# The attention output is turned by DMA transposes of a float16 pair instead of by TensorE

## The reference

```python
# layer 0
q = jnp.einsum('qc,bcn->bqn', Wq, xf)
k = jnp.einsum('qc,bcn->bqn', Wk, xf)
v = jnp.einsum('vc,bcn->bvn', Wv, xf)
attn = jax.nn.softmax(jnp.einsum('bqn,bqm->bnm', q, k) * scale, axis=-1)
out = jnp.einsum('bvm,bnm->bvn', v, attn).reshape(b, c, h, w)
y = gamma[0] * jnp.einsum('oc,bchw->bohw', Wo, out) + x
# layer 1, on y cut into 8 x 8 patches p
low = p.reshape(B * nP, C, 4, 2, 4, 2).mean(axis=(3, 5))
high = p - _up2_nearest(low)
low = _prelu(_bn(einsum('oc,nchw->nohw', mag_w, low) + mag_b), alpha)
hs = jnp.concatenate([high, jnp.roll(high, 1, axis=2)], axis=1)
hs = _prelu(_bn(einsum('oc,nchw->nohw', phase_w, hs) + phase_b), alpha)
out = _up2_nearest(low) + hs[:, :C]
```

## Time and profile before

| | us |
|---|---|
| median of 3 runs (2370.53 to 2370.84) | 2370.56 |
| span of the profiled execution | 2369.9 |
| PE busy | 2294.1 (97%) |
| DVE busy | 1784.5 (75%) |
| ACT busy | 1369.1 (58%) |
| POOL busy | 720.0 (30%) |

### The profile page before, as it was taken

The page is one execution under the profiler, slowest core; times in us unless marked ns, Lnnn a source line. Parts: engine busy times, 40 slices in busy tenths (PEclk is TensorE's granted clock), DMA queues, the critical chain, the costliest instruction groups (busy, mean ns, idle before and its releaser), DMA issues.

```text
span 2369.9 us, 48520 instructions
## 1 busy us (share of the span) xinstructions
PE 2294.1 (97%) x16885; PEld 1845.1 (78%) x16885; DVE 1784.5 (75%) x2838; ACT 1369.1 (58%) x2547; POOL 720.0 (30%) x891
## 2 busy tenths in 40 slices
PE   5799999999989999999999999999999999999997
PEld 4588888887878888888877888878887777777786
DVE  6777887777777777887776877777887777778764
ACT  3456665555655656665655655656665555565564
POOL 2232332232332232332232323232332223133222
PEclk7899999999999999999999999999999999999998
DMA  4201110000110001110000100000000000000000
GB/s 155 66 19 40 40 40 31 31 28 30 40 41 32 30 19 40 40 40 31 31 27 23 31 31 31 13 18 31 31 31 22 22 12 9 21 21 21 21 18 19
DMA packets 42119, 75.50 MB, mean 32 GB/s; under 512 B 4864, under 2 KB 6144, under 8 KB 42080
## 3 DMA queue, kind: packets, MB, share of 16 engines
q1 hardware_dynamic: 42080, 75.00, 9.8%
HBM read 55.59 MB, written 19.40 MB: 32 GB/s over the span
## 4 chain that ended last, share of the span: by engine, by line
PE 91%; issue 4%; DVE 2%; ACT 1%; POOL 1%; DMA 0%; SPq 0%; DVEq 0%; ACTq 0%; POOLq 0%
PE O L521 19%; PE O L523 18%; PE O L522 18%; PE M L374 14%; PE M L411 10%; PE S L482 10%; PE M L392 1%; ACT p L641 1%; DVE pl L899 1%; PE M L417 1%; DMA uh<-in_x 0%; DVE on L894 0%; POOL z L1052 0%; PE O L374 0%; ACT ph L638 0%
## 5 line engine op out<-in xcount | busy, mean ns | idle before, releaser
L521 PE MATMUL O<-uh,ph 128*128 128x257 f16 x4096 | 1136.0, 277 | 2.3 <-DVE pl L899 1.9
L523 PE MATMUL O<-uh,pl 128*128 128x257 f16 x4096 | 1122.6, 274 | 0.0
L522 PE MATMUL O<-ul,ph 128*128 128x256 f16 x4096 | 1119.8, 273 | 0.0
L638 ACT ACTIVATE ph<-S 128x512 f16<-128x512 f32 x1024 | 612.3, 598 | 705.0 <-PE S L482 704.4
L814 DVE TENSOR_REDUCE pmax<-M 128x1 f32<-128x512 f32 (+1 forms) x1024 | 679.7, 686 | 329.1 <-PE M L411 317.1
L899 DVE TENSOR_TENSOR pl<-p,ph 128x512 f16<-128x512 f32 x1024 | 782.1, 764 | 136.6 <-ACT p L641 131.3
L641 ACT ACTIVATE p<-S 128x512 f32<-128x512 f32 x1024 | 609.3, 595 | 0.8 <-DVE pl L899 0.2
L521 PEld LDWEIGHTS O<-uh,ph 128*128 128x128 f16 x4096 | 401.0, 98 | 263.2 <-issue 142.5
L482 PE MATMUL S<-qcur,kst 128*128 128x512 f32 x1024 | 486.0, 479 | 21.7 <-ACT p L641 16.9
L523 PEld LDWEIGHTS O<-uh,pl 128*128 128x128 f16 x4096 | 401.9, 98 | 51.2
L522 PEld LDWEIGHTS O<-ul,ph 128*128 128x128 f16 x4096 | 405.1, 99 | 38.9
(11 more groups left out here) (147 smaller groups left out, 1702.5 us busy)
## 6 DMA issues: line engine op xcount, KB each, us to landing
xr<-in_x SPq DMA_DIRECT2D x37, 512.0 KB, 3.6
out_y<-z SPq DMA_DIRECT2D x32, 512.0 KB, 2.8
xb<-in_x SPq DMA_DIRECT2D x25, 512.0 KB, 3.6
xs<-in_x SPq DMA_DIRECT2D x21, 512.0 KB, 3.7
qraw<-q_scratch SPq DMA_DIRECT2D x99, 64.0 KB, 1.8
ul<-in_x SPq DMA_DIRECT2D x4, 512.0 KB, 8.1
uh<-in_x SPq DMA_DIRECT2D x4, 512.0 KB, 8.7
q_scratch<-qsave SPq DMA_DIRECT2D x32, 64.0 KB, 1.6
```

Source lines behind the costliest of these rows:

```text
L521: nc.tensor.matmul(O[j][:, 0:UW], ph[:, t % 4, q], uh[parity][:, t, :], start=(t == 0), stop=False)
L522: nc.tensor.matmul(O[j][:, 0:C], ph[:, t % 4, q], ul[parity][:, t, :], start=False, stop=False)
L523: ins = nc.tensor.matmul(O[j][:, 0:UW], pl[:, t % 4, q], uh[parity][:, t, :], start=False, stop=(t == MT - 1))
L638: nc.scalar.activation(ph[:, t % 4, :], S[t % 2][:, :], ACT.Exp, scale=SCALE)
```

## The change

`normalise` writes the output as a float16 pair. `onh` is `oraw` times the reciprocal of the sum, rounded; `onl` is the same product less `onh`, rounded. The gain per image is no longer multiplied into `rs` but copied to `gcur`. A new `turn_out` on SP waits for the pair and issues two DMA transposes, `onh` to `yth` and `onl` to `ytl`, each of 128 x 1024 elements of two bytes, eight blocks of 128 x 128. They stand between the load of `xb` and the load of `xr`. The `y` tasks are gone from all plans and from PE. `add_residual` is now one block on DVE behind the tasks of step 6 (`RESIDUAL`): it waits for the transposes, multiplies `yth` by the gain and adds `xr` in two instructions, waits for these, and adds `ytl` times the gain in two more. Who waited for the `y` tasks (POOL's frequency split and SP's load of `xr`) waits for `y_ready`. Two output weights that were loaded through `on` get a buffer `wraw` of their own.

```diff
-FULL = Plan(steps_with_maxima({0: [("kq",), ("u", 0)], 2: [("u", 1)], 5: [("y", 0)], 6: [("y", 1)], 19: [("low", 0)],
+FULL = Plan(steps_with_maxima({0: [("kq",), ("u", 0)], 2: [("u", 1)], 19: [("low", 0)],
...
+            def turn_out(g):
+
+                sp.wait_ge(on_ready, g + 2)
+                sp.sem_inc(on_seen, 1)
+                for src, dst in ((onh, yth), (onl, ytl)):
+                    sp.dma_start_transpose(dst[:, :, :, :].rearrange("p j t q -> p (j t) q"),
+                                           src[:, :, :].rearrange("p j c -> p (j c)")).then_inc(on_turned, 16)
...
-                emptied(sp, plan, g, ("y", 1))
+                turn_out(g)
+                sp.wait_ge(y_ready, g + 1)
...
-                nc.vector.tensor_tensor(rs[:, :], rs[:, :], gain.to_broadcast([128, SUB]), ALU.mult).then_inc(rs_step, 1)
+                for j in range(SUB):
+                    ins = nc.vector.tensor_scalar(onh[:, j, :], oraw[:, j, 0:C], rs[:, j:j + 1], None, ALU.mult)
+                ins.then_inc(rs_step, 1)
+                nc.vector.tensor_copy(gcur[:, :], gain)
                 dve.wait_ge(rs_step, 2 * g + 2)
                 for j in range(SUB):
-                    ins = nc.vector.tensor_scalar(on[:, j, :], oraw[:, j, 0:C], rs[:, j:j + 1], None, ALU.mult)
+                    ins = nc.vector.scalar_tensor_tensor(onl[:, j, :], oraw[:, j, 0:C], rs[:, j:j + 1], onh[:, j, :],
+                                                         ALU.mult, ALU.subtract)
                 ins.then_inc(on_ready, 1)
...
+            def add_residual(g):
+
+                dve.wait_ge(on_turned, 32 * g + 32)
+                dve.wait_ge(xr_loaded, 16 * g + 16)
+                dve.wait_ge(high_ready, g + 1)
+                yv = [y[:, h, :, :].rearrange("p r w -> p (r w)").rearrange("p (j q) -> p j q", q=128) for h in range(CT)]
+                for h in range(CT):
+                    ins = nc.vector.scalar_tensor_tensor(yv[h], yth[:, :, h, :], gcur[:, 0:1],
+                                                         xr[:, h, :].rearrange("p (j q) -> p j q", q=128), ALU.mult, ALU.add)
+                ins.then_inc(y_half, 1)
+                dve.wait_ge(y_half, g + 1)
+                for h in range(CT):
+                    ins = nc.vector.scalar_tensor_tensor(yv[h], ytl[:, :, h, :], gcur[:, 0:1], yv[h], ALU.mult, ALU.add)
+                ins.then_inc(y_ready, 1)
...
+                    if t == RESIDUAL:
+                        add_residual(g)
```

More of the change, by code:

```diff
@@ L42 @@
 LEAD = 2
-ROUND_X, ROUND_CONV, SCAN, NEGATIVE = 9, 14, 12, 26
+ROUND_X, ROUND_CONV, SCAN, NEGATIVE, RESIDUAL = 9, 14, 12, 26, 6
 DOUBLE = (8, 10, 14, 16, 18, 22, 24, 26)
@@ L76, in steps_with_maxima @@
     return steps
-FULL = Plan(steps_with_maxima({0: [("kq",), ("u", 0)], 2: [("u", 1)], 5: [("y", 0)], 6: [("y", 1)], 19: [("low", 0)],
+FULL = Plan(steps_with_maxima({0: [("kq",), ("u", 0)], 2: [("u", 1)], 19: [("low", 0)],
                                20: [("low", 1)], 21: [("high", 0)], 23: [("high", 1)]}))
-LAST = Plan(steps_with_maxima({4: [("y", 0)], 5: [("y", 1)], 19: [("low", 0, 1)], 21: [("high", 0)], 23: [("high", 1)]},
+LAST = Plan(steps_with_maxima({19: [("low", 0, 1)], 21: [("high", 0)], 23: [("high", 1)]},
                               first=3, doubled=(6, 8, 10, 12, 14, 16, 18, 24, 25)),
             before=(FULL, ALL - NCH))
-FINAL = Plan({4: [("y", 0)], 5: [("y", 1)], 19: [("low", 0)], 20: [("low", 1)], 21: [("high", 0)], 23: [("high", 1)]},
+FINAL = Plan({19: [("low", 0)], 20: [("low", 1)], 21: [("high", 0)], 23: [("high", 1)]},
              before=(LAST, NCH - 1))
-TAIL = Plan({0: [("y", 0), ("y", 1), ("low", 0), ("low", 1), ("high", 0), ("high", 1)]}, before=(FINAL, 1))
+TAIL = Plan({0: [("low", 0), ("low", 1), ("high", 0), ("high", 1)]}, before=(FINAL, 1))
 MAXIMA_BY_KEYS = [(j, m) for m in range(NCH) for j in range(SUB)]
@@ L150, in attention_conv @@
         rs = sb("rs", [128, SUB])
-        on = sb("on", [128, SUB, C])
+        wraw = sb("wraw", [128, SUB, C])
+        onh, onl = [sb(n, [128, SUB, C], f16) for n in ("onh", "onl")]
+        yth, ytl = [sb(n, [128, SUB, CT, 128], f16) for n in ("yth", "ytl")]
+        gcur = sb("gcur", [128, 1])
         y = sb("y", [128, CT, ROWS, WID])
@@ L164, in attention_conv @@
         wraw_v = p32[:, 1, :].rearrange("p (t n) -> p t n", n=C)
-        wraw_o = on[:, 0:CT, :]
-        wraw_qk = on[:, CT:2 * CT, 0:2 * DQK]
+        wraw_o = wraw[:, 0:CT, :]
+        wraw_qk = wraw[:, CT:2 * CT, 0:2 * DQK]
         x0 = [buf.bitcast(f32)[:, 0:HW].rearrange("p (i t n) -> p i t n", t=CT, n=CH)
@@ L198, in attention_conv @@
         o02_out, o13_out, rs_step, on_ready = sem("o02_out"), sem("o13_out"), sem("rs_step"), sem("on_ready")
+        on_seen, on_turned, y_half, y_ready = sem("on_seen"), sem("on_turned"), sem("y_half"), sem("y_ready")
         pairs_ready, low_ready, high_ready = sem("pairs_ready"), sem("low_ready"), sem("high_ready")
@@ L251, in split_frequencies @@
         def split_frequencies(eng, ops, plan, g):
-            emptied(eng, plan, g, ("y", 1))
+            eng.wait_ge(y_ready, g + 1)
             for t in range(CT):
@@ L356, in _ @@
             turns(sp, turn)
+            turn_out(ALL)
             for o in range(CT):
@@ L365, in _ @@
             sp.wait_ge(qsave_free, 16 * (1 + ALL))
+            sp.wait_ge(on_turned, 32 * (1 + ALL))
         @block.tensor
@@ L386, in project_u @@
                                [[wu[v][:, t, :] for t in range(CT)] for v in range(2)])
[L387 to L392, removed]
                 return ins
@@ L492, in tasks @@
                         ins = project_kq(bank, (xbh, xbl)) if kind == "kq" else project_u(bank, (xbh, xbl), task[1])
-                    elif kind == "y":
-                        pe.wait_ge(on_ready, g + 2)
-                        ins = transposed(bank, task[1])
                     elif kind == "low":
@@ L559, in _ @@
                 pe.wait_ge(m_free[n % 2], use(TAIL, ALL, n))
[L560 to L563, removed]
+                if task[0] == "low":
                     pe.wait_ge(conv_in, ALL + 1)
@@ L715, in _ @@
             for n, task in TAIL.numbered[0]:
[L716 to L721, removed]
+                act.wait_ge(m_filled[n % 2], use(TAIL, ALL, n) + 1)
+                if task[0] == "low":
+                    norm_low(M[n % 2], ALL, task[1:], m_free[n % 2])
+                else:
+                    norm_high(M[n % 2], ALL, task[1], m_free[n % 2])
         @block.vector
@@ L927, in take @@
                         .then_inc(free, 1)
-                elif kind in ("y", "max", "negmax"):
+                elif kind in ("max", "negmax"):
                     dve.wait_ge(m_filled[n % 2], use(plan, g, n) + 1)
-                    if kind == "y":
-                        add_residual(bank, g, task[1], free)
-                    elif kind == "max":
+                    if kind == "max":
                         partial_max(bank, task[1], task[2], free)
@@ L979, in _ @@
             normalise(ALL)
-            for n, task in TAIL.numbered[0][:CT]:
-                dve.wait_ge(m_filled[n % 2], use(TAIL, ALL, n) + 1)
-                add_residual(M[n % 2], ALL, task[1], m_free[n % 2])
+            add_residual(ALL)
             split_frequencies(dve, nc.vector, TAIL, ALL)
```

## The result

The changed kernel takes 2468.84 us (median of 4 runs, 2462.05 to 2471.68), the kernel before 2370.7 beside it (4 runs, 2370.53 to 2371.02). The ratio is 1.0405, with a 95% interval of 1.0393 to 1.0417: slower by 4.1%. The prediction was 2455.5 with a range of 2400 to 2680; side and range hold, and the time came out 13 us higher.

The account below looks back on a forecast made before the run. PE, busy 97% of the span, was taken to bound the kernel. FULL chunks +62.9, LAST +16.9, FINAL -0.9 and tail +6.0 made +84.9 us on 2370.6, so 2455.5, range 2400 to 2680.

Parts of the forecast that it names:

- what goes from PE: Steps 5 and 6 of a chunk: four transposes leave each, 0.45 us per four, a gain of 0.90 us per chunk.
- the wait at `u`: Step 2 of a FULL chunk: DVE reaches `kst` 1.56 us later, so PE waits 0.81 before the second half of `u`.
- step 8: FULL chunk: PE waits for bank M0 behind DVE's maximum of step 7, 1.40 us for the block plus 1.31 for the landing.
- The two terms for the block and for the landing: Step 8 of a FULL chunk: block of four adds 1.40 us; DVE standing for transposes landing at 615.7 adds 1.31.
- LAST: Seven chunks: -0.90 from PE, +1.56 at `qst`, +1.75 in step 8, no landing wait; +2.41 us each, +16.9 together.
- FINAL: The one FINAL chunk: no maxima to be starved, so only PE's gain counts, -0.9 us.
- The tail: Finishing the last chunk's output: DMA wait, block of 2.90 us and `onl` of 1.56 lie open, +6.0 us in all.
- Issue by block: Rival on SP's queue: each transpose splits into 8 block issues, 16 a chunk; 2550 us, or 2682 at 0.69 each; chance 0.20.
- Block after block: Rival on the DMA queue: each of 16 blocks pays its own landing, 1.6 us, 25.6 together; 3085 us; chance 0.13.
- Absorbed: Rival at `kst` and behind step 6: 0.90 gain stays whole in 32 chunks, tail costs 6; -23, 2348 us; chance 0.07.

## Why the prediction was right, and where it was off

**Right: what goes from PE.** Steps 5 and 6 went from 2.25 to 1.80 and 1.81, 0.89 against 0.90.

**Right in kind, a little large: the wait at `u`.** 0.70 against 0.81, while `onh` stood at its 1.14 and `onl` at 1.67 for four, 0.43 apiece to the next start against 0.40. `kst` starts 1.29 later, not 1.56: the 0.26 that DVE waited behind `rs` in the earlier trace rows went with the multiply and was in no term. With the slack of 0.75 that alone would make the price 0.54. Two small things, in no term either, went the other way: 0.05 from the end of `kst` (624.89) to PE's start, and 0.11 by which the first four matmuls behind the wait took longer (0.58 to the next group instead of 0.47).

**Right in place, too large: step 8.** The start of the block was forecast at 614.36 if the data are there; in the trace DVE is ready at 633.65 + 0.69 = 634.34, less 19.99 is 614.35. Its length was 2.78 against 2.90. What failed is the landing. The two terms for the block and for the landing made 2.71, and the step grew by 2.20. The forecast had the second landing at 615.7 and DVE went on at 634.95 - 19.99 = 614.96, so it stood 0.61 instead of 1.31. Two errors partly met in that. The issues took 1.27 and 1.81 us instead of 0.39 each, so the second ended at 612.65 and not at 610.45. But both transposes do not wait for xb and then take 2.8 us: xb landed as forecast, at about 612.9 (628.99 + 3.9 - 19.99), and DVE went on 2.1 behind that, 2.3 after the second issue had ended. Less the 0.61, the step grew by 1.59, more than the block's 1.40: 0.14 of it lie between the end of the maximum (639.02) and PE's matmul (639.16), and were in no term.

**Missing: the clock.** The sum moved PE's work about at one speed. The changed kernel has 13 more stretches at 1.2 GHz; at 1.61 each that is some 21 us. It is the largest error, and it hid the two that were too large: the undisturbed FULL chunk is 2.15 longer (forecast 2.62), and with 9 of 21 disturbed the mean is about 2.8. The 24 FULL turns cost 70.3 where 62.9 was forecast; without the 11 falls in them, 17.7 us, they would have cost some 53. That the total was only 13 us off is in part luck.

**LAST.** The whole delay was to be paid at `qst`, 1.56, and 1.75 in step 8. One chunk's rows have 1.23 and 1.45 (the other six 1.36 to 1.37 and 1.44 to 1.53):

```profile
1889.39 0.51 PE L420 MATMUL M<-kst,qst 96*128 96x512 f32 x1 [1.23 <-DVE qst L812]
...
1901.03 0.51 PE L420 MATMUL M<-kst,qst 96*128 96x512 f32 x1 [1.45 <-DVE pmax L816]
```

There is no landing wait, as forecast. Five of the seven are 2.2 to 2.3 longer (forecast 2.41), two, with the clock down behind the wait for `qst`, 3.8.

**FINAL: the wrong sign.** "No maxima to be starved: -0.9" overlooked the other thing that DVE makes for PE. It is 1.4 longer; PE stands 1.26 and then 0.72 us for `pl`, which is queued behind `onl` and behind the block:

```profile
2381.01 0.28 PE L527 MATMUL O<-uh,ph 128*128 128x257 f16 x1 [1.26 <-DVE pl L905]
...
2389.73 0.28 PE L527 MATMUL O<-uh,ph 128*128 128x257 f16 x1 [0.72 <-DVE pl L905]
```

**The tail:** +6.6 against +6.0. From the issue of the first transpose (2437.77) to DVE's first add (2442.24) it is 4.47, forecast 3.68; the block took 2.86 and `onl` 1.67, as priced. Here nothing else is on the queue. The two issues took 1.25 and 1.34 instead of 0.39 each, 1.8 more than forecast; DVE went on 1.85 after the second had ended (2440.39) instead of 2.9, 1.0 less. So two errors partly met here too.

**The rivals.** *Issue by block* is half right: the issue of such a DMA does grow, to about 1.3 us and, for the second in a FULL turn, mostly 1.6 to 2.4 (2.8 once), not to 8 x 0.43 = 3.4, and it is hidden because SP has nothing urgent behind it (the kernel before with the DMAs added, 2370.21). *Block after block* is out: 16 blocks were there 4.47 us after the first issue began, 0.28 each. By that the 1309 ns that the Trainium skill (VectorE: DVE Perf Modes, The three transpose paths) has for one 128 x 128 is no price that adds up over the blocks of one DMA. Nor did the rate that the Trainium skill states (Advanced Engine Details and Errata, X-Bar Transpose (TRN2)) set the landing: by the estimate from it the 512 KB take 1.4 us, and the runs show medians of 3.1 to 4.3 us for each half of it. *Absorbed* named its conditions: under 0.75 us ahead of `kst`, under 1.50 behind step 6. The version with both spread meets them, and its sum was 2348 where 2347.9 was measured; against the kernel before beside it that is a gain of 23.7 where 22.8 was forecast.

**Not settled:** what makes the clock fall after one idle time and not after another of the same length. In FULL chunks 1.2 to 1.3 us brought no fall; in the changed kernel, with 1.81 to 2.37 us (3.23 once), it fell in 11 of 24, and the idle times with and without a fall overlap; 3.1 brought one in each. In LAST chunks it fell after 1.37 us of waiting for `qst` in two of seven and not after 1.36 in another, while with `onl` spread none of the seven single gaps of 1.51 to 1.59 brought one; the windows behind the two (the first of 1.40 us, the second of 3.40):

```profile
2030.60:2032.00 1.40, 1.40 (x8) 1.01 (x6) 0.87 (x2) 0.00 (x0) 0.00 (x0) 0.50 0.49 119
```

```profile
1960.20:1963.60 3.40, 3.40 (x28) 2.56 (x26) 2.77 (x5) 1.43 (x4) 0.00 (x0) 1.00 0.73 154
```

No run varied the idle time alone, so the length that matters, if it is the length, was not measured. The price of a fall rests on the stores of the outputs, the number of falls on the granted clock; that the idle times bring them rests on where they stand: behind the gaps, and gone with the gaps in the versions that spread the work.

## What to carry to other kernels

A helper engine's spare share does not by itself say whether work fits on it: look in its queue for the instructions that another engine waits for, and put new work in pieces smaller than the slack behind each of them. Moving eight of VectorE's instructions a chunk, and the issue of one DMA, with no change to what they compute, turned a loss of 4.1% into a gain of 1.0%. When you price an idle time of TensorE, add what it does to its clock afterwards, and when an engine's work feeds several others, go through the list of all its readers in every variant of the loop, the last one too.

## What the runs showed of the hardware

- **A transposing DMA is slow to issue.** SP's queue was busy for about 1.3 us with a 128x1024 float16 transpose within the core's memory, and for 1.6 to 2.4 (2.8 once) with the second of a FULL turn of the changed kernel, against 0.40 for the 512 KB load of xb. From issue to landing (medians) it took 4.2 to 4.3 and 3.8 to 4.0 us behind xb's load, 3.2 and 3.1 where it went first. In the page of the changed kernel 74560 packets are under 512 bytes; before it was 4864.
- **It disturbed nobody here.** 64 of them, unused, left the kernel before at a ratio of 0.9993.
- **TensorE's clock halves behind short idle times.** The granted clock was 0.51 for 3.4 us behind idle times of PE of about 2 us, in 11 of 24 FULL chunks, at 1.61 us each; in every chunk with 3.1 us of standing; and in no FULL chunk with 1.2 to 1.3, though in two LAST chunks of the changed kernel behind 1.37. The length alone does not tell them apart.
